# Column sums of the first attention's probabilities: key blocks added on GpSimd, products moved on TensorE

## The chip, the cores and the metric

The kernel runs on one core of a Trainium2 chip. Time is device microseconds of one execution of the whole program. Three runs of the kernel before gave 2255.92, 2256.36 and 2256.59 us (median 2256.36). The engines are TensorE (PE, with PEld for its weight loads), VectorE (DVE), ScalarE (ACT), GpSimd (POOL) and SyncE (SP), which issues the DMAs of this stage.

## The reference, cut to what matters

The program is a decoder block of two cross attentions and two feed-forward parts on x of (8, 256, 512). The change is in the first attention, of 16 heads of 32 over 256 context tokens (of the reference's context only the first 257 rows count as image tokens, and there are 256):

```python
q = rms_norm(linear(x, q_w, q_b), norm_q_w).reshape(B, L, NH, HD)
k_img = rms_norm(linear(ctx_img, k_img_w, k_img_b), norm_k_img_w).reshape(B, -1, NH, HD)
v_img = linear(ctx_img, v_img_w, v_img_b).reshape(B, -1, NH, HD)
...
scores = jnp.einsum('bqhd,bkhd->bhqk', q, k) * scale
probs = jax.nn.softmax(scores, axis=-1)
return jnp.einsum('bhqk,bkhd->bqhd', probs, v)
```

x here is layer-normalised before, and the output is projected, scaled by tanh of a gate and added to x.

## The kernel before

The function is `image_attention` (tiles with the prefix `a_`). It runs in turns, one for a batch i of 256 tokens (two blocks t of 128), for i from -2 to 7. The order on every engine is written out by hand in one loop over the turns; semaphores tie the engines. In the turn of batch i the attention of i is finished while the normalisation, queries, keys and values of i+1 and the keys of i+2 are made.

Projections are three f32 products for each of four parts of 128 (high and low parts of both operands, lines 50 to 52), twelve for a block of 128 tokens and 512 outputs: `queries` (reads a_xt), `values` and `keys` (read a_ctx). The 16 heads are handled in four groups c of four heads (j). `scores` (L740) makes the scores with queries on the partitions, for the maximum (`find_peak`, L1147). `turned_scores` (L755, L758) makes them again with keys on the partitions and takes the maxima off; it fills four double blocks `abc_banks`, so that group c+1 can start only when `exponentials` (L954, ScalarE, two instructions of two heads each) has read group c. The probabilities lie in `a_prob` [128 keys, 2 buffers, 4 heads, 2 key blocks t, 256 queries], buffer c mod 2. `weigh` (L772) multiplies them with the values: 8 products of 32 rows. `masses(i, h, r)` (L782) sums them over the keys with a matrix of ones, `picks_share`; r is the group's place within half h (h = 0: groups 0 and 1; h = 1: groups 2 and 3), and both key blocks are summed by accumulation in the bank m0 or m1, 8 products a group. VectorE inverts the sums (`invert`, L1154, RECIPROCAL 1.75 us), `inverses` (L795) spreads them over the partitions, `divide` (L1159) applies them, ScalarE and GpSimd split the result in a high and a low part (`output_high` L966, `output_low` L614), and `outputs` projects it.

All of these products but the scores and `weigh` go through a ring of three PSUM banks, `a_ring`, in the order of the list PLACES; a user waits until the bank's last user has been read.

What stands in program order around the change:
- ScalarE: exponentials 0, squares of the keys of i+1 (two), exponentials 1, square of query block 0, weight pieces, square of query block 1 (`square_query`, L939), exponentials 2, `output_raw` (L960), weight pieces, `context_high` (L904), exponentials 3, high parts of keys and queries (L920, L924), weight pieces (L976, L982, L984, in the turns up to batch 3 only) and outputs. The pieces are parts of the next stage's weights, made ready here.
- VectorE: low part of x, values' bias (`value`, L1126), statistics of i+2 and a chain of ten tiny instructions for the inverse square roots (`key_scales`: L1096, L1099, L82, and L85, L87, L89 three times, about 0.2 us a step), bias of query block 0 (L1126), `scale_keys` (L1109), `normalise` (L1089) of i+2, bias of query block 1, `query_scales` (L1115 and the like chain), `scale_queries` (L1122), `invert` 0, bias of value block 1, low parts of keys (L1140), `divide` 0, low parts of queries (L1140), `invert` 1.
- GpSimd: `add_row` (L609, two instructions, behind `normalise`), `context_low` (L604), `output_low` twice.

## Time and profile before

| | |
|---|---|
| median of the runs | 2256.36 us |
| the profiled execution, span | 2257.6 us (the page gives no other time of it) |
| PE busy in the span | 2145.6 us, 95% |
| DVE, ACT, POOL busy | 1307.3, 1078.4, 677.1 us |
| first attention | to about 430 us; turned peaks (L721) of batches 0 to 7 at 53.66, 102.67, 159.74, 211.14, 257.56, 304.00, 350.43, 399.04 us |
| L782, the sums | 512 records for 256 products, 0.38 us each, several at a time side by side |

In the page's slices each digit is a tenth of busy time in a fortieth of the span. The first seven slices are this stage: PE 6999998, and PEclk, the granted clock, 9 throughout, since a slice is longer than its dips. A timeline row merges like instructions: its time reaches from the first start to the last end, and the number behind x is the count. Since each f32 product stands in two records, x16 is eight products.

### The profile page before, as it was taken

How to read it: one execution, taken by the hardware profiler on the slowest of the kernel's cores; microseconds unless marked ns; L12 is line 12 of the kernel's file. 1: busy time of each engine (PE TensorE's matmuls, PEld its weight loads, DVE VectorE, ACT ScalarE, POOL GpSimd, SP SyncE). 2: the span in 40 equal slices, each digit the busy share in tenths (PEclk: the TensorE clock that was granted, in tenths of full speed). 3: DMA queues.
4: the chain of work that ended last, by engine and by line, in shares of the span. 5: the costliest groups of instructions: out<-in, count | busy, mean ns of one | idle time of the engine just before them, and what ended most of it. 6: DMA issues, size and time to landing. Idle time of an engine off the chain costs nothing. (4 is left out here: it accounts for less than half of the span.)

```text
span 2257.6 us, 43111 instructions
## 1 busy us (share of the span) xinstructions
PE 2145.6 (95%) x17918; PEld 1788.6 (79%) x17918; DVE 1307.3 (58%) x2283; ACT 1078.4 (48%) x1887; POOL 677.1 (30%) x684
## 2 busy tenths in 40 slices
PE   6999998899999999999999999999799999899996
PEld 5666666444489999999999999999677877799995
DVE  7666776689854445444544444454555455767764
ACT  4676633478744444333433344333455554425553
POOL 4111210266512221111111111211255543125664
PEclk9999999999999999999999999999999999999998
DMA  7454202100032222321223123221000000258995
GB/s 261 160 170 134 81 11 113 57 1 1 29 131 108 89 100 106 112 75 64 86 94 113 64 87 119 79 70 49 25 2 2 2 2 30 85 187 262 275 274 103
DMA packets 46931, 215.30 MB, mean 95 GB/s; under 512 B 6161, under 2 KB 6161, under 8 KB 32401
## 3 DMA queue, kind: packets, MB, share of 16 engines
q1 hardware_dynamic: 29968, 139.13, 17.1%
q0 software_dynamic: 16768, 73.41, 11.3%
q8 instruction: 143, 2.34, 0.4%
q14 instruction: 52, 0.42, 0.1%
HBM read 169.00 MB, written 43.52 MB: 94 GB/s over the span
## 5 line engine op out<-in xcount | busy, mean ns | idle before, releaser
L336 POOL TENSOR_TENSOR c_prob<-c_prob,c_inv_mass 128x512 f32<-128x512 f32 x128 | 130.5, 1039 | 353.1 <-DVE c_inv_mass L328 353.1
L318 ACT ACTIVATE c_prob<-abc_banks,c_neg_peak 128x256 f32<-128x256 f32 x256 | 117.7, 472 | 178.0 <-DVE c_neg_peak L310 178.0
L50 PE MATMUL abc_banks<-c_ctx,c_wk_hi 128*128 128x256 f32 x512 | 146.6, 286 | 2.3 <-DVE c_qt_lo L2148 2.3
L50 PE MATMUL abc_banks<-bc_xt,bc_wq_hi 128*128 128x256 f32 x512 | 147.7, 288 | 0.0
L51 PE MATMUL abc_banks<-bc_xt,bc_wq_hi 128*128 128x256 f32 x512 | 144.9, 283 | 0.0
L52 PE MATMUL abc_banks<-bc_xt,bc_wq_lo 128*128 128x256 f32 x512 | 144.8, 283 | 0.0
L51 PE MATMUL abc_banks<-c_ctx,c_wk_hi 128*128 128x256 f32 x512 | 143.8, 281 | 0.0
L52 PE MATMUL abc_banks<-c_ctx,c_wk_lo 128*128 128x256 f32 x512 | 143.6, 281 | 0.0
L231 PE MATMUL abc_banks<-ab_wq,b_xqt 128*128 128x512 bf16 x512 | 117.2, 380 | 5.8 <-DVE b_h L202 3.7
L1898 POOL DMA_DIRECT2D c_ctx<-kept_scratch x24 | 13.2, 551 | 347.0 <-PE abc_banks L52 347.0
L3220 POOL DMA_INDIRECT out<-el_r,e_target x44 | 82.8, 1882 | 75.6 <-DMA out<-el_r,e_target 60.6
L2150 DVE TENSOR_TENSOR c_v_lo<-abc_banks,c_v_hi 128x512 fp32r<-128x512 f32 x64 | 44.3, 692 | 104.3 <-ACT c_v_hi L2067 104.3
L50 PE MATMUL abc_banks<-c_w_lo,c_o_hi 128*128 128x512 f32 x256 | 102.0, 398 | 2.4 <-DVE c_o_lo L382 2.4
L1343 POOL TENSOR_TENSOR b_hw<-b_h,b_lnw 128x512 f32<-128x512 f32 x64 | 80.9, 1274 | 73.9 <-DVE b_h L202 67.3
L51 PE MATMUL abc_banks<-c_w_hi,c_o_hi 128*128 128x512 f32 x256 | 101.9, 398 | 0.0
L52 PE MATMUL abc_banks<-c_w_hi,c_o_lo 128*128 128x512 f32 x256 | 101.7, 397 | 0.0
L50 PE MATMUL abc_banks<-c_w_lo,c_ctx 128*128 128x512 f32 x256 | 101.7, 397 | 0.0
L52 PE MATMUL abc_banks<-c_w_hi,c_ctx 128*128 128x512 f32 x256 | 101.3, 396 | 0.0
L51 PE MATMUL abc_banks<-c_w_hi,c_ctx 128*128 128x512 f32 x256 | 101.2, 395 | 0.0
L231 PEld LDWEIGHTS abc_banks<-ab_wq,b_xqt 128*128 128x128 bf16 x512 | 47.4, 98 | 66.8 <-DVE b_h L202 12.2
L2067 ACT ACTIVATE c_v_hi<-abc_banks 128x512 fp32r<-128x512 f32 x64 | 38.2, 597 | 127.7 <-PE abc_banks L52 127.7
L50 PEld LDWEIGHTS abc_banks<-c_ctx,c_wk_hi 128*128 128x128 f32 x512 | 96.4, 188 | 2.4 <-issue 2.4
(564 smaller groups left out, 7192.4 us busy)
## 6 DMA issues: line engine op xcount, KB each, us to landing
x_res<-b_w SPq DMA_DIRECT2D x48, 512.0 KB, 4.7
bc_xt<-kept_scratch POOLq DMA_DIRECT2D x24, 1024.0 KB, 5.1
c_ctx<-kept_scratch POOLq DMA_DIRECT2D x24, 1024.0 KB, 5.1
e_raw<-e_w SPq DMA_DIRECT2D x15, 1536.0 KB, 9.2
bc_raw<-c_w SPq DMA_DIRECT2D x16, 1024.0 KB, 4.9
h_res<-e_w SPq DMA_DIRECT2D x7, 1536.0 KB, 9.6
kept_scratch<-bc_xt SPq DMA_DIRECT2D x8, 1024.0 KB, 3.9
kept_scratch<-c_ctx SPq DMA_DIRECT2D x8, 1024.0 KB, 3.9
```

Source lines behind the costliest of these rows:

```text
L50: pe.matmul(out, lhs[0], rhs[1], start=first, stop=False)
L51: pe.matmul(out, lhs[0], rhs[0], start=False, stop=False)
L52: return pe.matmul(out, lhs[1], rhs[0], start=False, stop=last)
L231: mm = pe.matmul(ps[:, k % 2, :], self.xqt[:, n // 2 % 2, c, n % 2, :], w[:, c, self.quarter(k)], start=c == 0, stop=c == C - 1)
L318: ins = act.activation(self.prob[:, u % 2, j, :], self.s_ps[:, j, :], ACT.Exp, bias=self.neg_peak[:, u % 2, j:j + 1], accum_out=self.mass[ ...
L336: pool.tensor_tensor(part, part, self.inv_mass[:, u % 2, js].unsqueeze(2).to_broadcast([P, 2, SEQ]), ALU.mult).then_inc(self.prob_done, 1)
L1343: pool.tensor_tensor(hw[:, n % 2, cols], h[n % 2][:, cols], lnw[:, cols], ALU.mult).then_inc(hw_done, 1)
L1898: pool.dma_start(rows_of(both), kept[1, s % BATCH]).then_inc(ctx_kept_in, 16)
L2067: act.activation(front(k)[0], bank_of(f"f{k}", s), ACT.Copy, scale=SCALE if k < 2 else 1.0).then_inc(front_hi_done, 1)
L2150: ins = dve.tensor_tensor(low, bank_of(f"f{k}", s), f32(high), ALU.subtract)
L3220: pool.indirect_dma_start(out=out[:, :], out_offset=bass.IndirectOffsetOnAxis(ap=target[:, TB * j + t:TB * j + t + 1], axis=0), in_=r[:, j ...
```

## The change

On GpSimd a new function adds, for each group, the probabilities of the two key blocks into `both`, which lies in the tile `a_early_raw` (used only at the start before): two instructions of 128x512 (two heads), each behind the half of the exponential that it reads. `masses` multiplies this sum instead of both blocks: 4 products a group instead of 8. Both groups of a half are now summed at one place: the first half behind the scores of group 3, the second where it was. The wait of the exponentials for a free buffer is now on the additions and the product with the values. The bank of m0 and that of the values' second block change places in the ring, and so do `invert` 0 and the bias of that block on VectorE. Line numbers of the changed kernel are higher by 9 to 20 in this function.

```diff
--- before.py
+++ after.py
@@ -446,6 +446,7 @@
         k_sum, q_sum = sb("k_sum", [P, TB]), sb("q_sum", [P, TB])
         junk = sb("junk", [P, D], BF16)
         raw_v = early_raw[:, :, :, :].rearrange("p a j s -> p (a j s)").rearrange("p (c n) -> p c n", c=C)
+        both = early_raw
         raw = prob[:, :, :, :, :].rearrange("p a j t s -> p a (j t s)").rearrange("p a (c n) -> p a c n", c=C)
         s_ps = handed.s_ps
         x_turned = early.x_bank.bitcast(F16).rearrange("p (c t q) -> p c t q", c=C, t=TB)
@@ -466,7 +467,7 @@
         xn_done, xt_hi_done, k_hat_done, q_hat_done = sem("xn_done"), sem("xt_hi_done"), sem("k_hat_done"), sem("q_hat_done")
         kt_hi_done, qt_hi_done, k_squared, q_squared = sem("kt_hi_done"), sem("qt_hi_done"), sem("k_squared"), sem("q_squared")
         s_ready, peak_done, st_ready, exp_done = sem("s_ready"), sem("peak_done"), sem("st_ready"), sem("exp_done")
-        mass_half, w_ready = sem("mass_half"), sem("w_ready")
+        halves_added, w_ready = sem("halves_added"), sem("w_ready")
         o_raw_done, o_hi_done, o_lo_done = sem("o_raw_done"), sem("o_hi_done"), sem("o_lo_done")
         row_added, x_done, kx_steps, q_steps, stats_done = (
             sem("row_added"), sem("x_done"), sem("kx_steps"), sem("q_steps"), sem("stats_done"))
@@ -481,7 +482,7 @@
 
         TURNS = range(-2, BATCH)
         FIRST_PLACES = (("q0", 1), ("q1", 1), ("v0", 1), ("v1", 1))
-        PLACES = (("mt", 0), ("xt0", 1), ("v0", 1), ("xt1", 1), ("mean", -1), ("q0", 1), ("q1", 1), ("m0", 0), ("v1", 1), ("kt0", 1),
+        PLACES = (("mt", 0), ("xt0", 1), ("v0", 1), ("xt1", 1), ("mean", -1), ("q0", 1), ("q1", 1), ("v1", 1), ("m0", 0), ("kt0", 1),
                   ("kt1", 1), ("n0", 0), ("qt0", 1), ("qt1", 1), ("m1", 0), ("k0", 2), ("n1", 0), ("k1", 2), ("o0", 0), ("o1", 0))
         use_of = {("xt0", 0): 0, ("xt1", 0): 1}
         for i in TURNS:
@@ -613,6 +614,17 @@
                 pool.wait_ge(o_hi_done, 2 * i + h + 1)
                 pool.tensor_tensor(o_lo[:, 2 * h:2 * h + 2, :], o_f[:, :, :], f32(o_hi[:, 2 * h:2 * h + 2, :]),
                                    ALU.subtract).then_inc(o_lo_done, 1)
+
+            def add_halves(i, c):
+
+                n = C * i + c
+                if n >= 2:
+                    await_ready(pool, f"m{(n - 2) % C // 2}", (n - 2) // C)
+                for half in range(2):
+                    js = slice(2 * half, 2 * half + 2)
+                    pool.wait_ge(exp_done, 2 * n + half + 1)
+                    pool.tensor_tensor(both[:, n % 2, js, :], prob[:, n % 2, js, 0, :], prob[:, n % 2, js, 1, :],
+                                       ALU.add).then_inc(halves_added, 1)
 
             pool.memset(eps[:, :], RMS_EPS).then_inc(eps_done, 1)
             pool.memset(ones[:, :], 1.0)
@@ -650,8 +662,14 @@
                     pool.tensor_tensor(w_lo[WO][:, :, :], raw[:, 0], f32(w_hi[WO][:, :, :]), ALU.subtract).then_inc(w_lo_done[WO], 1)
                     pool.wait_ge(row_done, 2)
                     add_row(0)
+                if here(i):
+                    add_halves(i, 0)
+                    add_halves(i, 1)
                 if i >= -1 and here(i + 2):
                     add_row(i + 2)
+                if here(i):
+                    add_halves(i, 2)
+                    add_halves(i, 3)
                 if i >= 0 and here(i + 2):
                     context_low(i + 2)
                 if here(i):
@@ -773,20 +791,16 @@
                                        start=t == 0, stop=t == TB - 1)
                 mm.then_inc(w_ready, 1)
 
-            def masses(i, h, r):
+            def masses(i, h):
 
                 def emit(bank):
-                    n = C * i + 2 * h + r
-                    for t in range(TB):
+                    for r in range(2):
+                        n = C * i + 2 * h + r
+                        pe.wait_ge(halves_added, 2 * n + 2)
                         for j in range(4):
-                            mm = pe.matmul(bank[HD * j:HD * (j + 1), 0:SEQ], share[:, r, :], prob[:, n % 2, j, t, :],
-                                           start=r == 0 and t == 0, stop=r == 1 and t == TB - 1)
+                            mm = pe.matmul(bank[HD * j:HD * (j + 1), 0:SEQ], share[:, r, :], both[:, n % 2, j, :], start=r == 0, stop=r == 1)
                     return mm
-                if r == 0:
-                    pe.wait_ge(ring_free[use_of[f"m{h}", i] % BANKS], use_of[f"m{h}", i] // BANKS)
-                    emit(bank_of(f"m{h}", i)).then_inc(mass_half, 1)
-                else:
-                    use(f"m{h}", i, emit)
+                use(f"m{h}", i, emit)
 
             def inverses(i, h):
 
@@ -840,14 +854,13 @@
                 if i >= 0 and nxt:
                     queries(i + 1, 1)
                 if now:
-                    masses(i, 0, 0)
                     turned_scores(i, 2)
                     weigh(i, 1)
-                    masses(i, 0, 1)
                 if i >= 0 and nxt:
                     values(i + 1, 1)
                 if now:
                     turned_scores(i, 3)
+                    masses(i, 0)
                     weigh(i, 2)
                 if nxt:
                     turn_keys(i + 1, 0)
@@ -861,8 +874,7 @@
                     turn_queries(i + 1, 0)
                     turn_queries(i + 1, 1)
                 if now:
-                    masses(i, 1, 0)
-                    masses(i, 1, 1)
+                    masses(i, 1)
                 if i == BATCH - 1:
                     pe.wait_ge(early.ident_done, 1)
                     early.turn_x(pe, 0, x_turned)
@@ -945,10 +957,7 @@
                     act.wait_ge(w_lo_done[WO], 1)
                 if n >= 2:
                     act.wait_ge(w_ready, n - 1)
-                    if c % 2 == 0:
-                        act.wait_ge(mass_half, n // 2)
-                    else:
-                        await_ready(act, f"m{(n - 2) % C // 2}", (n - 2) // C)
+                    act.wait_ge(halves_added, 2 * (n - 1))
                 for half in range(2):
                     js = slice(2 * half, 2 * half + 2)
                     act.activation(prob[:, n % 2, js], s_ps[:, js], ACT.Exp).then_inc(exp_done, 1)
@@ -1233,10 +1242,10 @@
                     scale_queries(i + 1)
                 if i == -1:
                     value(i + 1, 0)
+                if nxt:
+                    value(i + 1, 1)
                 if now:
                     invert(i, 0)
-                if nxt:
-                    value(i + 1, 1)
                 if nxt:
                     low("kt", i + 1, 0, kt_lo, kt_hi, kt_hi_done)
                     low("kt", i + 1, 1, kt_lo, kt_hi, kt_hi_done)
```

TensorE, from the end of the scores of group 3 in the turn of batch 0 to the second half's sums. Before:

```order
L758 MATMUL abc_banks<-a_peak_t,picks_pick 128x256 x4
L772 MATMUL a_o_ps<-a_prob,a_v 32x256 x8
L674 MATMUL a_ring<-ident,a_kf 128x128 x4
L772 MATMUL a_o_ps<-a_prob,a_v 32x256 x8
L674 MATMUL a_ring<-ident,a_kf 128x128 x4
L795 MATMUL a_ring<-a_inv_mass,picks_spread 128x256 x2
L674 MATMUL a_ring<-ident,a_qf 128x128 x8
L782 MATMUL a_ring<-a_prob,picks_share 32x256 x16
```

Now, where L801 is `masses`, L790 `weigh`, L773 and L776 `turned_scores`, L692 the turned keys and queries and L809 `inverses`:

```order
L776 MATMUL abc_banks<-a_peak_t,picks_pick 128x256 x4
L801 MATMUL a_ring<-a_early_raw,picks_share 32x256 x8
L790 MATMUL a_o_ps<-a_prob,a_v 32x256 x8
L692 MATMUL a_ring<-ident,a_kf 128x128 x4
L790 MATMUL a_o_ps<-a_prob,a_v 32x256 x8
L692 MATMUL a_ring<-ident,a_kf 128x128 x4
L809 MATMUL a_ring<-a_inv_mass,picks_spread 128x256 x2
L692 MATMUL a_ring<-ident,a_qf 128x128 x8
L801 MATMUL a_ring<-a_early_raw,picks_share 32x256 x8
```

The sums of groups 0 and 1 stand in one group of 8 in front of `weigh` of group 2, and the 16 products of the second half are 8. (Before, 8 each stood in front of and behind the scores of group 2.)

GpSimd, one turn (the row additions of i+2 to the next). Before:

```order
L609 TENSOR_TENSOR x_res<-x_res,a_row 128x512 [waits a_xn_done]
L609 TENSOR_TENSOR x_res<-x_res,a_row 128x512
L604 TENSOR_TENSOR a_ctx_lo<-a_ctx_f,a_ctx_hi 128x1024 [waits a_ring_ready,a_ctx_hi_done]
L614 TENSOR_TENSOR a_o_lo<-a_o_f,a_o_hi 128x512 [waits a_o_hi_done] x2
L609 TENSOR_TENSOR x_res<-x_res,a_row 128x512 [waits a_xn_done]
```

Now, from group 0's additions on, where L626 are the additions, L610 `add_row`, L605 `context_low` and L615 `output_low`:

```order
L626 TENSOR_TENSOR a_early_raw<-a_prob 128x512 [waits a_exp_done,a_ring_ready]
L626 TENSOR_TENSOR a_early_raw<-a_prob 128x512 [waits a_exp_done]
L626 TENSOR_TENSOR a_early_raw<-a_prob 128x512 [waits a_exp_done,a_ring_ready]
L626 TENSOR_TENSOR a_early_raw<-a_prob 128x512 [waits a_exp_done]
L610 TENSOR_TENSOR x_res<-x_res,a_row 128x512 [waits a_xn_done]
L610 TENSOR_TENSOR x_res<-x_res,a_row 128x512
L626 TENSOR_TENSOR a_early_raw<-a_prob 128x512 [waits a_exp_done,a_ring_ready]
L626 TENSOR_TENSOR a_early_raw<-a_prob 128x512 [waits a_exp_done]
L626 TENSOR_TENSOR a_early_raw<-a_prob 128x512 [waits a_exp_done,a_ring_ready]
L626 TENSOR_TENSOR a_early_raw<-a_prob 128x512 [waits a_exp_done]
```

Four additions stand in front of the row additions and four between them and the low part of the context. The third and fourth group's wait for the ring (a_ring_ready) too, for the first half's sums, which read the buffer that they write.

## Rows read from the trace of the kernel before

**Rows 1.** Busy time by engine in one stretch of the first attention (us, x instructions).

```profile
250.00:300.00 50.00, 48.53 (x514) 34.92 (x510) 36.35 (x59) 21.45 (x32) 8.24 (x6) 1.00 0.13 43
```

**Rows 2.** TensorE's waits, batches 0 to 7: total us, times, longest.

```profile
PE a_o_ps L772 <- ACT a_prob L954: 5.1, 8, 1.4
```

**Rows 3.** Timeline of TensorE, batch 4: start, us, line, tiles, count, [idle before].

```profile
271.25 1.07 PE L782 MATMUL a_ring<-a_prob,picks_share 128*32 128x256 f32 x16
272.25 0.39 PE L755 MATMUL abc_banks<-a_qt_hi,a_kt_lo 32*128 32x256 f32 x4
...
274.29 1.05 PE L782 MATMUL a_ring<-a_prob,picks_share 128*32 128x256 f32 x16
275.26 0.50 PE L50 MATMUL a_ring<-ab_wq,a_ctx_hi 128*128 128x512 f32 x1
...
278.26 0.39 PE L755 MATMUL abc_banks<-a_qt_hi,a_kt_lo 32*128 32x256 f32 x4
...
281.52 1.07 PE L772 MATMUL a_o_ps<-a_prob,a_v 128*32 128x256 f32 x16 [0.45 <-ACT a_prob L954]
...
285.24 1.93 PE L782 MATMUL a_ring<-a_prob,picks_share 128*32 128x256 f32 x32
287.11 0.39 PE L740 MATMUL abc_banks<-a_kt_lo,a_qt_hi 32*128 32x256 f32 x4
```

**Rows 4.** Timeline of ScalarE, batch 4.

```profile
267.38 1.94 ACT L954 ACTIVATE a_prob<-abc_banks 128x1024 f32<-128x1024 f32 x2 [0.70 <-PE abc_banks L758]
...
273.31 0.63 ACT L939 ACTIVATE a_junk<-a_qf 128x512 bf16<-128x512 f32 x1 [2.11 <-DVE a_qf L1126]
...
273.94 1.92 ACT L954 ACTIVATE a_prob<-abc_banks 128x1024 f32<-128x1024 f32 x2
...
278.43 1.06 ACT L904 ACTIVATE a_ctx_hi<-a_ctx_f 128x1024 fp32r<-128x1024 f32 x1 [2.08 <-PE a_ring L52]
279.53 1.94 ACT L954 ACTIVATE a_prob<-abc_banks 128x1024 f32<-128x1024 f32 x2
```

**Rows 5.** Timeline of VectorE, batch 4.

```profile
268.56 0.17 DVE L85 TENSOR_TENSOR a_kx_tmp<-a_kx_rstd 128x4 f32<-128x4 f32 x1
...
269.74 0.69 DVE L1126 TENSOR_TENSOR a_qf<-a_ring,a_row 128x512 f32<-128x512 f32 x1
...
272.59 0.69 DVE L1126 TENSOR_TENSOR a_qf<-a_ring,a_row 128x512 f32<-128x512 f32 x1
274.06 1.24 DVE L1115 SCALAR_TENSOR_TENSOR a_q_var<-a_q_sum,a_eps 128x2 f32<-128x2 f32 x1 [0.79 <-ACT a_junk L939]
...
285.15 1.52 DVE L1140 TENSOR_TENSOR a_qt_lo<-a_ring,a_qt_hi 128x512 fp32r<-128x512 f32 x2
```

**Rows 6.** Timeline of GpSimd, batch 4.

```profile
272.75 2.54 POOL L609 TENSOR_TENSOR x_res<-x_res,a_row 128x512 f32<-128x512 f32 x2 [21.98 <-DVE a_xn L1089]
279.56 2.37 POOL L604 TENSOR_TENSOR a_ctx_lo<-a_ctx_f,a_ctx_hi 128x1024 fp32r<-128x1024 f32 x1 [4.28 <-ACT a_ctx_hi L904]
```

**Rows 7.** Timelines of VectorE and GpSimd, 9 to 12.5 us.

```profile
9.32 1.28 DVE L87 SCALAR_TENSOR_TENSOR a_kx_tmp<-a_kx_tmp,a_kx_var 128x4 f32<-128x4 f32 x1
10.63 1.20 DVE L89 SCALAR_TENSOR_TENSOR a_kx_rstd<-a_kx_tmp,a_kx_rstd 128x4 f32<-128x4 f32 x1
...
9.32 2.49 POOL L642 TENSOR_TENSOR a_ctx_lo<-a_ctx_f,a_ctx_hi 128x512 fp32r<-128x512 f32 x2
```

**Rows 8.** Timeline of ScalarE, batch 3.

```profile
233.18 1.92 ACT L954 ACTIVATE a_prob<-abc_banks 128x1024 f32<-128x1024 f32 x2
```

**Rows 9.** Timeline of TensorE, two waits of batches 2 and 6.

```profile
184.65 1.07 PE L772 MATMUL a_o_ps<-a_prob,a_v 128*32 128x256 f32 x16 [1.39 <-ACT a_prob L954]
...
390.72 0.79 PE L50 MATMUL a_ring<-a_w_lo,a_o_hi 128*128 128x512 f32 x1 [1.60 <-POOL a_o_lo L614]
...
395.23 0.39 PE L740 MATMUL abc_banks<-a_kt_lo,a_qt_hi 32*128 32x256 f32 x4
```

**Rows 10.** Busy time and granted clock behind the second of them.

```profile
392.00:394.00 2.00, 2.00 (x6) 1.52 (x6) 0.00 (x0) 0.00 (x0) 0.00 (x0) 0.50 0.00 0
```


## The prediction

> **What bounds the kernel now.** I read the stretches of the span first, then TensorE's waits, then the timelines of one turn of the first attention (batch 4's, from its turned peaks at 257.56 us on) for TensorE, ScalarE, VectorE and GpSimd, and last the places where VectorE and GpSimd meet. The change touches the first attention alone, up to about 430 us. In a steady stretch of it TensorE is busy 48.53 of 50 us and GpSimd 8.24 [rows 1], so a product taken from TensorE is time, unless what it feeds comes later. TensorE's wait for a finished exponential, 5.1 us in eight turns, is the one that the change works next to [rows 2]. In the turn of batch 4 the reader is to see how tight two places are. (a) The third scores start at 278.26 [rows 3]; they need the third exponential, which ScalarE runs from 273.94 to 275.86 (two halves, 1.92) straight behind the square of the queries at 273.31, and that waits for VectorE's biased queries at 272.59 [rows 4, 5]. (b) The next scores start at 287.11, only 0.44 us behind the end of the last low part of the queries on VectorE, 285.15 + 1.52 = 286.67 [rows 3, 5]. Behind (b) the turn runs as now, whatever came before it.
>
> **What is taken from TensorE.** Each column sum was 8 products (16 records) over both key blocks and becomes 4 (8 records). The first two sums take 272.25 - 271.25 = 1.00 and 275.26 - 274.29 = 0.97 us, the last two together 287.11 - 285.24 = 1.87 [rows 3]. Sixteen records for two sums then cost 0.97 both times: 1.00 + 0.97 - 0.97 = 1.00 in the first part of a turn, 1.87 - 0.97 = 0.90 in the second, 1.90 a turn, 15.2 us over eight. That is the ceiling if nothing waits.
>
> **Where the moved products stand.** Without the two sums in front, TensorE is ready for the third scores at 278.26 - 1.00 - 0.97 = 276.29. These need the third exponential's end, 275.86 now: 0.4 to spare. The first two sums now stand behind them, in the stretch in which TensorE waited 0.45 for the last exponential [rows 3].
>
> **What GpSimd adds.** Eight additions of 128x512 a turn. Its row addition of that shape and type took 2.54 for two, 1.27 each [rows 6]; the nearest other row is the low part of the context, 2.37 for twice the elements, 1.19 [rows 6]. I take 1.27, 10.2 us a turn; the rows' own ends are 1.19 and 1.27, and only more than these would matter (a rival below). GpSimd has the room; the question is who else is held. No DMA is issued or moved.
>
> **The addition and VectorE.** Where GpSimd begins an addition while VectorE is in its chain of tiny instructions on two SBUF operands, they stop: at 9.32 GpSimd runs two back to back for 2.49, and VectorE's 0.16 us instructions take 1.28 and 1.20, one behind each [rows 7]. In batch 4's turn the query-scale instruction at 274.06, as tiny as those, takes 1.24, till GpSimd's row additions end at 275.29 [rows 5, 6]. Now look where the second exponential's additions fall. It starts at 267.38, its halves end at about 268.40 and 269.32 [rows 4]; additions run 268.4 to 269.7 and to 270.95. VectorE's inverse square root is in its middle then: the step at 268.56 would wait till 269.7, the next till 270.95, and the rest follows as now; at 0.2 a step, the step of 268.96 stands at 271.0. The chain ends 2.0 us late, and with it the biased queries (269.74, then 272.59 becomes 274.6), the square (275.35), and the third exponential (276.0 to 277.9) [rows 4, 5]. TensorE, ready at 276.3, waits 1.6 us at the third scores and starts them at 277.95 instead of 278.26.
>
> **Rule beside it.** The Trainium skill (SBUF — State Buffer, Who interferes with whom) says that a VectorE instruction with two SBUF inputs and a GpSimd one that reads SBUF exclude each other for the whole instruction, and one with an input in PSUM is free. The rows at 9.32 agree for the first half. It would also let VectorE's f32 scalings hold off GpSimd, which no row here shows; the sum below leaves that out.
>
> **The turns.** Batches 4 and 5: third scores 277.95 to 279.1, context part on ScalarE 278.4 to 279.45, last exponential at 279.45 against 279.53 [rows 4], the sums fill the gap, the last product with values at 281.5 against 281.52. Nothing won so far. The third and fourth additions wait until the first sums are through (280.1, for the buffer): 280.1 to 285.3, just in time for the second pair of sums at 285.24 + 0.5, and context's low part ends at 287.6. At (b) the low queries end as now, so the new gain is 0.44 of the 0.90. I take -0.5 each. Batches 0, 2 and 3: between the third exponential and the last one ScalarE also does the weight pieces and the context (batch 3's last exponential starts at 233.18 with no idle time in front, behind both [rows 8]), so the 2.0 us pass through to the last exponential and to (b): 2.0 - 0.44 = +1.6 each; in 0 and 2 ScalarE's pieces behind it carry nearly all of it, +1.8 and +2.1. Batch 1's chain is over before its second exponential ends; it wins a part of the first 1.0: -0.7 (estimate). Batch 6 has no tokens left to normalise, its exponential stays in time, and both gains arrive: -2.2 (1.90 and part of the 0.45). Batch 7 has no other work: each addition stands in the path, and what the 1.90 brings they mostly take: -0.5 (estimate). Sum: 1.8 - 0.7 + 2.1 + 1.6 - 0.5 - 0.5 - 2.2 - 0.5 = +1.1 us. The profiled execution's span is 2257.6 us, 1.2 over the median of the runs, 2256.36; the change is read from the one and put on the other: 2257.5.
>
> **Rivals.**
> *Chain not held (faster).* If VectorE's chain slips through (additions begin a step later, or only one step is held), batches 4 and 5 win 0.44 + 1.6 = 2.1 each, 6 wins 2.5, 0, 2, 3 win 0.44 each (ScalarE still sets the last exponential), 1 and 7 win 1.0 each: -10.0, 2246.3. For it: at the meeting point the two start within 0.2 us of each other, and a step that comes first is through. Against: the instructions at 9.32, 10.63 and 274.06 all waited in full, and six more steps follow.
> *The clock falls (slower).* The place is the new 1.6 us wait in front of the third scores. A wait of 1.60 was followed by half clock, products at 390.72 on taking 4.51 till 395.23 against 278.26 - 275.26 = 3.00 for twelve at full clock [rows 3, 9], granted clock 0.50, which is 1.2 GHz [rows 10]; a wait of 1.39 alone was not (1.07 for 16 records, as ever) [rows 9]. Price 1.5 each. It decides if the new waits count as the 1.60 did: in batches 4 and 5 in full, in 0, 2, 3 partly behind ScalarE: 3.0 + 4.5 x 0.6 = +5.7, in all +6.8, 2263.2.
> *GpSimd comes late (slower).* The additions are queued ahead of the low context, and that ahead of the low outputs; the keys product waits for the context. My sum leaves 0.1 to 0.4 us there. At 1.6 us an addition (each held off by VectorE's scalings) four cost 1.3 more, in batches 4 to 7 in full: +5, 2262.5.
>
> **Numbers.** Forecast 0.45 (own range 2253 to 2261.5), chain not held 0.23, clock 0.20, GpSimd late 0.12. 0.2% is 4.5 us, about what a measurement can tell. Faster: the second case and a rest of the first, 0.25; within: most of the first, a fifth of the last two, 0.45; slower 0.30. The range takes in the -10 case at its edge and the clock case: 2246 to 2265.
>
> **What would show it.** Right: 128 products for the sums instead of 256; five turns in which a 128x4 step of VectorE takes 1.2 us twice just behind the second exponential; a wait of TensorE for the exponential in front of the third scores (none there now) of 1.6 us; turns of 46.4 us still at 46, batch 3's longer by 1.6, batch 6's shorter by 2. Wrong: those steps at 0.16 us throughout (then the time falls by 10), half clock behind the new waits, or the keys products waiting for the low context.

## The result, and the profile of the changed kernel

The changed kernel takes 2270.89 us in the median of four runs (2264.82 to 2273.48), the kernel before 2256.14 beside it (2255.68 to 2256.59): a ratio of 1.0059, with a 95% interval of 1.0045 to 1.0073. Measured once more later, with twelve runs, it is 2264.46 against 2256.91, 1.0031 (1.0018 to 1.0044). So it is slower, by some 7 to 15 us; the forecast of 2257.5 was too low, and the first measurement lies above its range, which ended at 2265. The second lies just inside, with a change of 7.6 us where 1.1 was forecast.

The span of the profiled execution is 2271.8 us, 14.2 more than before. ScalarE and TensorE run the same instructions at both kernels' ends, so the two traces can be laid on each other. I read two marks: where the first attention ends (the last of its output products but one starts) and how long the last stage, the experts, takes (ScalarE's first to last write of `el_r`). The first attention ends at 436.25 instead of 429.34, +6.9. Between there and the last stage both take 1620.4. The last stage, whose code is not touched, takes 196.15 instead of 189.66, +6.5; 0.8 more lie behind its last write. Two causes, then; the first is that of the change.

Busy time in the stretch of [rows 1], in the changed kernel:

```profile
250.00:300.00 50.00, 47.22 (x497) 34.46 (x494) 39.26 (x60) 24.91 (x35) 18.12 (x14) 1.00 0.27 84
```

TensorE has lost 1.3 us of work and GpSimd has gained 10. TensorE's waits over the first attention, of which [rows 2] showed the third kind:

```profile
PE abc_banks L773 <- ACT a_prob L963: 12.6, 8, 2.1
PE a_ring L50 <- POOL a_o_lo L615: 10.0, 6, 5.1
PE a_o_ps L790 <- ACT a_prob L963: 6.3, 5, 1.9
```

The first of them, turned scores that wait for an exponential, was 2.2 us in two waits before. Now batch 4's turn, which starts at 266.28 here. VectorE and GpSimd, as in [rows 5, 6]:

```profile
277.06 0.16 DVE L89 SCALAR_TENSOR_TENSOR a_kx_rstd<-a_kx_tmp,a_kx_rstd 128x4 f32<-128x4 f32 x1
277.26 1.27 DVE L85 TENSOR_TENSOR a_kx_tmp<-a_kx_rstd 128x4 f32<-128x4 f32 x1
278.56 1.22 DVE L87 SCALAR_TENSOR_TENSOR a_kx_tmp<-a_kx_tmp,a_kx_var 128x4 f32<-128x4 f32 x1
279.82 0.16 DVE L89 SCALAR_TENSOR_TENSOR a_kx_rstd<-a_kx_tmp,a_kx_rstd 128x4 f32<-128x4 f32 x1
...
283.45 0.68 DVE L1135 TENSOR_TENSOR a_qf<-a_ring,a_row 128x512 f32<-128x512 f32 x1
```

```profile
277.21 2.55 POOL L626 TENSOR_TENSOR a_early_raw<-a_prob 128x512 f32<-128x512 f32 x2 [1.96 <-ACT a_prob L963]
283.61 2.52 POOL L610 TENSOR_TENSOR x_res<-x_res,a_row 128x512 f32<-128x512 f32 x2 [3.85 <-DVE a_xn L1098]
289.10 4.98 POOL L626 TENSOR_TENSOR a_early_raw<-a_prob 128x512 f32<-128x512 f32 x4 [2.97 <-ACT a_prob L963]
294.03 2.40 POOL L605 TENSOR_TENSOR a_ctx_lo<-a_ctx_f,a_ctx_hi 128x1024 fp32r<-128x1024 f32 x1
```

Two steps of VectorE's chain wait one addition each, exactly as the prediction placed them; the second biased queries stand 17.17 us into the turn instead of 15.03. The third exponential and TensorE follow (ScalarE as in [rows 4], TensorE as in [rows 3]):

```profile
284.17 0.63 ACT L951 ACTIVATE a_junk<-a_qf 128x512 bf16<-128x512 f32 x1 [2.11 <-DVE a_qf L1135]
...
284.80 1.92 ACT L963 ACTIVATE a_prob<-abc_banks 128x1024 f32<-128x1024 f32 x2
```

```profile
286.76 0.39 PE L773 MATMUL abc_banks<-a_qt_hi,a_kt_lo 32*128 32x256 f32 x4 [1.62 <-ACT a_prob L963]
...
287.92 1.07 PE L801 MATMUL a_ring<-a_early_raw,picks_share 128*32 128x256 f32 x16
...
295.66 0.39 PE L758 MATMUL abc_banks<-a_kt_lo,a_qt_hi 32*128 32x256 f32 x4 [0.50 <-DVE a_qt_lo L1149]
```

TensorE waits 1.62 us before the third scores, and the turn is 46.0 us long instead of 46.4.

The lengths of the eight turns (from one batch's turned peaks to the next's, the last to the end mark), over two executions of each kernel:

| | b0 | b1 | b2 | b3 | b4 | b5 | b6 | b7 | end of first attention | last stage |
|---|---|---|---|---|---|---|---|---|---|---|
| before | 49.0 | 57.1 | 51.4 | 46.4 | 46.4 | 46.4 | 48.6 | 30.3 | 429.3 | 189.7 |
| before, again | 48.9 | 56.6 | 50.5 | 46.4 | 46.4 | 46.4 | 48.8 | 28.9 | 427.1 | 195.4 |
| changed | 49.7 | 58.3 | 56.0 | 48.1 | 46.0 | 46.1 | 46.6 | 31.4 | 436.3 | 196.2 |
| changed, again | 49.9 | 58.7 | 55.3 | 49.5 | 46.1 | 46.1 | 46.2 | 29.6 | 433.9 | 189.7 |
| change of the means | +0.8 | +1.7 | +4.7 | +2.4 | -0.4 | -0.3 | -2.3 | +0.9 | +6.9 | |
| predicted | +1.8 | -0.7 | +2.1 | +1.6 | -0.5 | -0.5 | -2.2 | -0.5 | +1.1 | |

The ends differ by 0.5 us less than the sum of the turns (+7.4), because the first peaks start at 53.66 and 54.19 before and at 54.20 and 52.53 in the changed kernel. Batches 4, 5 and 6 came out as predicted, batch 0 is 1.0 better and batch 3 0.8 worse. Batches 1, 2 and 7 make most of the 6 us that the sum missed.

The same eight turns can be split by what TensorE does: idle, or busy, and of its busy time what the granted clock cost it (each busy stretch times one minus the clock granted in it). In the means of two traces each:

| | idle | lost to the clock while busy | the rest |
|---|---|---|---|
| before | 28.2 | 14.1 | 332.0 |
| changed | 47.1 | 18.0 | 316.6 |
| change | +18.9 | +3.9 | -15.4 |
| predicted | +16.3 (1.1 + 15.2) | 0 | -15.2 |

The work that was taken away is what was predicted. The miss is 3.9 us of clock and 2.6 of waiting. Batch 1, VectorE and GpSimd:

```profile
121.16 0.69 DVE L1135 TENSOR_TENSOR a_qf<-a_ring,a_row 128x512 f32<-128x512 f32 x1
121.76 3.17 DVE L1118 SCALAR_TENSOR_TENSOR a_kf<-a_kf,a_kx_rstd,a_row 128x512 f32<-128x512 f32 x2
```

```profile
121.38 3.01 POOL L626 TENSOR_TENSOR a_early_raw<-a_prob 128x512 f32<-128x512 f32 x2 [4.19 <-ACT a_prob L963]
```

The chain is over there when the second exponential ends, as I had said; but the two scalings of the keys stand behind it, and they take 3.17 instead of 1.41 (two of 0.74, one starting 0.66 behind the other), and the additions 3.01 instead of 2.55: each engine waits for the other. Batch 2 of the changed kernel, ScalarE and behind it GpSimd and TensorE:

```profile
202.56 1.15 ACT L993 ACTIVATE x_res<-x_res,a_shifts 128x1024 bf16<-128x1024 f32 x1
205.57 1.24 ACT L991 ACTIVATE x_res<-x_res,a_shifts,a_inv_mean 128x1024 f32<-128x1024 f32 x1 [1.86 <-DMA x_res<-b_w]
206.85 1.15 ACT L993 ACTIVATE x_res<-x_res,a_shifts 128x1024 bf16<-128x1024 f32 x1
207.90 0.61 ACT L975 ACTIVATE a_o_hi<-a_o_f 128x512 fp32r<-128x512 f32 x1
```

```profile
208.59 1.26 POOL L615 TENSOR_TENSOR a_o_lo<-a_o_f,a_o_hi 128x512 fp32r<-128x512 f32 x1 [7.88 <-ACT a_o_hi L975]
```

```profile
209.91 0.80 PE L50 MATMUL a_ring<-a_w_lo,a_o_hi 128*128 128x512 f32 x1 [5.05 <-POOL a_o_lo L615]
```

A weight piece (`x_res<-b_w`) has not landed when ScalarE asks for it, and the high output, its low part and TensorE's last products are queued behind. Before, ScalarE went from one piece to the next without a gap there, and TensorE's wait was 2.75. The piece is not late because ScalarE is: between the issue of its load and ScalarE's asking for it lie 4.64 us here (199.07 to 203.71) and 4.56 before (193.94 to 198.50). The load itself took 6.5 us instead of 4.4.

### The profile page after: what moved, and what is told of

It reads as the page before. It is cut to its first block and busy times, and to the rows that moved or that the text cites. A ratio compares the mean times of both kernels' runs of the same rounds, so it can differ in the third digit from the quotient of the medians.

```text
span 2271.8 us, 42690 instructions
## 1 busy us (share of the span) xinstructions
PE 2134.3 (94%) x17643; PEld 1784.7 (79%) x17662; DVE 1324.1 (58%) x2283; ACT 1077.3 (47%) x1887; POOL 756.5 (33%) x748
## 5 line engine op out<-in xcount | busy, mean ns | idle before, releaser
L626 POOL TENSOR_TENSOR a_early_raw<-a_prob 128x512 f32<-128x512 f32 x64 | 80.9, 1291 | 161.0 <-ACT a_prob L963 148.7
L1352 POOL TENSOR_TENSOR b_hw<-b_h,b_lnw 128x512 f32<-128x512 f32 x64 | 80.9, 1274 | 74.8 <-DVE b_h L202 67.4
```

Source lines behind the costliest of these rows:

```text
L626: pool.tensor_tensor(both[:, n % 2, js, :], prob[:, n % 2, js, 0, :], prob[:, n % 2, js, 1, :], ALU.add).then_inc(halves_added, 1)
L1352: pool.tensor_tensor(hw[:, n % 2, cols], h[n % 2][:, cols], lnw[:, cols], ALU.mult).then_inc(hw_done, 1)
```

## The experiments

Ends and turns are read as in the table above, each from one profiled execution; the ratios are to the kernel before on the same chip.

**Additions of the second group behind the row addition.** On GpSimd:

```diff
                     add_halves(i, 0)
-                    add_halves(i, 1)
                 if i >= -1 and here(i + 2):
                     add_row(i + 2)
                 if here(i):
+                    add_halves(i, 1)
                     add_halves(i, 2)
```

> The changed kernel, with the additions of the second head group queued behind GpSimd's row addition instead of ahead of it; nothing else. Theory (held chain): GpSimd's additions hold VectorE's inverse square root for 2.0 us in batches 0, 2, 3, 4 and 5, and with it the third exponential. Here the additions stand some 7 us later, when that chain is over: its steps take 0.16 us, the wait of 1.6 us in front of the third scores is gone in batches 4 and 5, and the first attention ends 8 to 12 us sooner than in the changed kernel. Rival (GpSimd is late, or the products' new place costs): nothing is sooner, the first sums wait more, the end moves by +2 to -2. Last stage: it grew by 6.5 us in the changed kernel; if that comes from what the new sums round to, it stays here (time 2259 to 2263); if it comes from when the stage is reached or from chance, it may be gone (2252 to 2256).

Measured: 2293.4 us, ratio 1.0159 (1.0114 to 1.0204); the first attention ends at 465.3, 29 us later than in the changed kernel. Batch 4's turn is 53.1 us. Neither theory had this; VectorE's timeline has where it starts, and GpSimd's beside it.

```profile
296.31 1.25 DVE L1124 SCALAR_TENSOR_TENSOR a_q_var<-a_q_sum,a_eps 128x2 f32<-128x2 f32 x1 [0.79 <-ACT a_junk L951]
297.59 1.23 DVE L82 TENSOR_SCALAR a_q_rstd<-a_q_var 128x2 int32<-128x2 int32 x1
298.85 1.21 DVE L85 TENSOR_TENSOR a_q_tmp<-a_q_rstd 128x2 f32<-128x2 f32 x1
...
303.53 1.18 DVE L89 SCALAR_TENSOR_TENSOR a_q_rstd<-a_q_tmp,a_q_rstd 128x2 f32<-128x2 f32 x1
304.75 3.93 DVE L1131 TENSOR_SCALAR a_qf<-a_qf,a_q_rstd 128x512 f32<-128x512 f32 x2
```

```profile
295.00 2.54 POOL L610 TENSOR_TENSOR x_res<-x_res,a_row 128x512 f32<-128x512 f32 x2 [6.20 <-DVE a_xn L1098]
297.49 2.55 POOL L626 TENSOR_TENSOR a_early_raw<-a_prob 128x512 f32<-128x512 f32 x2
300.96 4.95 POOL L626 TENSOR_TENSOR a_early_raw<-a_prob 128x512 f32<-128x512 f32 x4 [0.92 <-PE a_ring L801]
305.88 2.51 POOL L605 TENSOR_TENSOR a_ctx_lo<-a_ctx_f,a_ctx_hi 128x1024 fp32r<-128x1024 f32 x1
```

The first chain is free here (0.16 us a step), and the third exponential in time. But the queries have a chain of their own, 16.5 us into a turn, which I had left out: six of its steps wait for an addition (the first for one of the rows, as before), and the two scalings of the queries, which read one SBUF tile and a scalar, take 3.93 instead of 0.89. TensorE then waits 6.1 us in this turn for what VectorE has queued behind them (27.3 us over five turns). Part of the 29 us is clock: while TensorE is busy it loses 33.8 us to it in the eight turns, against 19.6 in the changed kernel's first trace. So a hold costs what is behind it; a later place is not a safer one.

**The additions alone.** The kernel before, with `add_halves` and its places as in the change (result unused), and in `exponentials`:

```diff
                     act.wait_ge(w_ready, n - 1)
+                    act.wait_ge(halves_added, 2 * (n - 1))
```

> The kernel before, with GpSimd's additions put in where the changed kernel has them, their result unused, and the exponentials waiting for them as there; products and order on TensorE as before. Theory (held chain): the third exponential comes 2.0 us late; TensorE still has its two sums in front of the third scores, so batches 4 and 5 lose little (0 to 0.5), batches 0, 2 and 3, where ScalarE sets the last exponential, 1.6 to 2.1 each: the first attention ends 5 to 8 us later than before. Rival (the additions cost nothing by themselves, the order of the products does): no more than +1. Last stage: the sums are the same as before, so if it grows with what the sums round to it is as before (total 2261 to 2264); if it grows from the time at which it is reached, it is longer here too (2266 to 2271).

Measured: 2286.07 us, ratio 1.0129 (1.0096 to 1.0161); the end is at 454.9, 26 us later than before, not 5 to 8. Half of the theory holds (the first chain loses its two steps), but without the sums' bank to wait for, GpSimd takes up the third group's additions as soon as the third exponential ends, which is in the second chain: it is over 28.1 us into the turn instead of 19.7. In the changed kernel a wait that I had priced at nothing, for the first sums before the third group's additions, keeps them out of that chain. Here too the clock is a part: 23.9 us lost while busy, against 14.5. The last stage took 189.7, though it was reached late.

**No additions.** The changed kernel with GpSimd's part and all waits on it taken out, and:

```diff
-                        pe.wait_ge(halves_added, 2 * n + 2)
+                        pe.wait_ge(halves_added, 1)
```

> The changed kernel without the additions: the 128 products for the sums read a tile that GpSimd fills once with a constant, and nothing waits for additions. What is left out: the real sums of the probabilities. Theory (held chain): TensorE keeps its 1.90 us a turn and VectorE's chain is free: turns of 44.3 us in batches 4 and 5 instead of 46.4, the first attention ends 8 to 12 us sooner than in the kernel before and 15 to 19 sooner than in the changed one. Rival (the order or the banks of the products cost): the end stays within 4 us of the kernel before. The last stage isn't compared, since other numbers reach its routing.

Measured: 2258.54 us, ratio 1.0011 (0.999 to 1.0031). The end is at 425.6, only 3.8 us sooner than before, which by its number is the rival's outcome, and 10.7 sooner than in the changed kernel. But its turns start 4.3 us later (the first peaks at 57.93 instead of 53.66; GpSimd's one fill of the whole tile is the only new work ahead of them), and together they are 8.1 us shorter than in the first trace of before. Batches 4 and 5 take 45.5, not 44.3. The low part of the context now starts 20.1 us into the turn instead of 22.0, and meets the scaling of the queries:

```profile
279.65 3.06 DVE L1115 TENSOR_SCALAR a_qf<-a_qf,a_q_rstd 128x512 f32<-128x512 f32 x2
```

```profile
280.05 2.38 POOL L605 TENSOR_TENSOR a_ctx_lo<-a_ctx_f,a_ctx_hi 128x1024 fp32r<-128x1024 f32 x1 [2.42 <-ACT a_ctx_hi L901]
```

The same hold, by an instruction that has always been there. Batch 2 takes 52.4 us, more than before: its weight piece is late as well (6.2 us for the load, 1.5 of ScalarE's wait), though nothing holds the chain. The last stage took 199.3, but other numbers reach it.

**Fills in place of additions.**

```diff
-                    pool.tensor_tensor(both[:, n % 2, js, :], prob[:, n % 2, js, 0, :], prob[:, n % 2, js, 1, :],
-                                       ALU.add).then_inc(halves_added, 1)
+                    pool.memset(both[:, n % 2, js, :], 2.0).then_inc(paced, 1)
+                    pool.wait_ge(paced, 2 * n + half + 1)
+                    pool.memset(both[:, n % 2, js, :], 2.0).then_inc(halves_added, 1)
```

> The changed kernel with each addition of 128x512 replaced by two fills of the same 128x512 piece of the tile, 0.53 us each: GpSimd has the same queue, the same waits and writes, and is busy some 1.1 to 1.2 us for each instead of 1.27, but reads nothing from SBUF. What is left out: the real sums. Theory (held chain, by GpSimd's reading against VectorE's instructions with two SBUF operands): VectorE's steps are free or held by less, and the first attention ends as without the additions, within 3 us. Rival (GpSimd is late, or everything waits for its queue): it ends as in the changed kernel, within 3 us. A third outcome: writes hold VectorE as reads do, then the steps take 0.5 us or more and the end is between.

Measured: 2249.41 us, ratio 0.998 (0.9958 to 1.0002). Batches 4 and 5 take 44.37, and the end is at 416.1: 20 us before the changed kernel's, and 9.5 before that of the run without additions, not within 3 of it (6 of the 9.5 lie ahead of the first peaks). In the chain of batch 4:

```profile
262.92 0.16 DVE L89 SCALAR_TENSOR_TENSOR a_kx_rstd<-a_kx_tmp,a_kx_rstd 128x4 f32<-128x4 f32 x1
263.12 0.16 DVE L85 TENSOR_TENSOR a_kx_tmp<-a_kx_rstd 128x4 f32<-128x4 f32 x1
```

```profile
262.79 0.53 POOL L627 MEMSET a_early_raw<- 128x512 f32 x1 [2.68 <-ACT a_prob L965]
```

GpSimd is nearly as busy (1.1 us instead of 1.27 for each), in the same queue with the same waits, and writes the same tile, and VectorE's steps take 0.16. So neither GpSimd's queue nor its writes hold the steps with two SBUF operands; what the addition does besides, and the fill does not, is to read SBUF. The rule of the Trainium skill (SBUF — State Buffer, Who interferes with whom) that they meet only where the GpSimd instruction reads agrees. It also takes GpSimd's lateness out as a cause. Over the eight turns this kernel is 10.1 us shorter than the mean of before, which is the total that the rival "chain not held" had worked out (-10.0). In batches 4, 5 and 6 that is its mechanism (-2.0, -2.0 and -2.4 against 2.1, 2.1 and 2.5); the rest agrees by luck, since batch 1 wins 3.5 where it had 1.0, and batch 2 loses 1.9 where it had a gain of 0.4. Batch 2 has the late piece again (6.5 us for the load, a wait of 1.8), with its exponentials in time.

**The second group's sum by products.** Only the first, third and fourth group are added; the first sums stand in front of the last turned scores.

```diff
+                        if n % C == 1:
+                            for t in range(TB):
+                                for j in range(4):
+                                    mm = pe.matmul(bank[HD * j:HD * (j + 1), 0:SEQ], share[:, r, :], prob[:, n % 2, j, t, :],
+                                                   start=False, stop=t == TB - 1)
+                            continue
...
+                    masses(i, 0)
                     turned_scores(i, 3)
-                    masses(i, 0)
```

> The changed kernel, but the second head group isn't added by GpSimd: its sum takes 8 products over both key blocks as before, the other three groups 4 each; both first sums stand in front of the last turned scores. Theory (only the second group's additions meet VectorE's first chain, 11 us into a turn; those of groups 1, 3 and 4 stand beside instructions that read PSUM): the steps there take 0.16 us again, the third exponential is in time, batches 0 and 3 to 5 are 0.4 to 1.5 us shorter than before, the first attention ends 2 to 8 us before that of the kernel before and 9 to 15 before the changed kernel's. Rival (the other additions, the order or the weight pieces' DMAs cost as well): the end is at or behind the kernel before. The last stage should be 189.7 or some 196 us, whichever chance gives.

Measured: 2253.18 us, ratio 0.9981 (0.997 to 0.9993); turns of 48.1, 54.1, 51.2, 45.9, 45.4, 45.5, 47.3 and 28.8, the end at 418.9: 17 us before the changed kernel's first trace and 10 before that of before, both more than expected. The chain's steps take 0.16 throughout, and TensorE's waits for exponentials are short again:

```profile
PE a_ring L50 <- POOL a_o_lo L616: 8.5, 7, 3.2
PE a_o_ps L792 <- ACT a_prob L974: 5.4, 8, 1.1
PE abc_banks L760 <- DVE a_qt_lo L1160: 3.5, 7, 0.5
```

The eight turns together take 366.4 us, 15.3 less than in the changed kernel and 2.2 more than with fills, though TensorE has four products more in each. Two of the eight additions of a turn, then, carry the loss; the sums' place was moved as well, and I did not try that alone. Batch 2 has no wait of 5 us here either, because the load of its piece took 4.9 us and had landed when ScalarE asked. That is not owed to exponentials in time: they are so in the last two runs too, and there it was late.

**Small pieces.** The second group's two additions cut into eight of 128x128:

```diff
+                    if c == 1:
+                        for j in (2 * half, 2 * half + 1):
+                            for part_of in (slice(0, SEQ // 2), slice(SEQ // 2, SEQ)):
+                                ins = pool.tensor_tensor(both[:, n % 2, j, part_of], prob[:, n % 2, j, 0, part_of],
+                                                         prob[:, n % 2, j, 1, part_of], ALU.add)
```

> The changed kernel with the second group's two additions of 128x512 cut into eight of 128x128 each 0.3 to 0.45 us. Theory (a step of VectorE waits for the addition that runs, and GpSimd's next one is in before VectorE's next step): two waits of 1.2 us become six to eight of 0.3 to 0.4; each still lets one step through, so the chain loses 0.9 to 1.6 us instead of 2.1, and the first attention ends 2 to 6 us sooner than in the changed kernel. Rival (the chain waits till GpSimd's queue is empty): nothing is won, or it is longer by the pieces' fixed costs.

Measured: 2257.99 us, ratio 1.0002 (0.9989 to 1.0015), the end at 431.4, 5 us sooner than the first trace of the changed kernel. Batches 4 to 6 win; batches 1 and 2 (58.9 and 55.5) do not.

```profile
276.52 0.46 DVE L85 TENSOR_TENSOR a_kx_tmp<-a_kx_rstd 128x4 f32<-128x4 f32 x1
277.01 0.39 DVE L87 SCALAR_TENSOR_TENSOR a_kx_tmp<-a_kx_tmp,a_kx_var 128x4 f32<-128x4 f32 x1
277.43 0.39 DVE L89 SCALAR_TENSOR_TENSOR a_kx_rstd<-a_kx_tmp,a_kx_rstd 128x4 f32<-128x4 f32 x1
```

```profile
276.50 3.39 POOL L629 TENSOR_TENSOR a_early_raw<-a_prob 128x128 f32<-128x128 f32 x8 [1.98 <-ACT a_prob L970]
```

One step passes behind each piece, as the theory said: six waits of 0.2 to 0.3, 1.4 us in all, and TensorE waits 0.85 at the third scores instead of 1.62. The hold is by instruction.

**The changed kernel again**, unchanged.

> The changed kernel once more, unchanged. If the 6.5 us that its last stage took longer in the first trace were chance of that execution, the last stage is 189 to 191 us here and the time 2262 to 2266; if they belong to this kernel, 196 again and 2269 to 2273. The first attention should end at 436 within 1 us in both.

Measured: the 2264.46 us given at the start, the end at 433.9 (2.3 sooner than in the first trace, more than I had allowed), the last stage 189.7.

**Row additions last.** The version with the second group by products, and GpSimd's two row additions behind its low outputs.

```diff
                     output_low(i, 1)
+                if i >= 0 and here(i + 2):
+                    add_row(i + 2)
```

> The version without the second group's additions, and GpSimd's two row additions of a turn queued behind its low outputs instead of in the middle. Theory (a GpSimd instruction that reads SBUF holds VectorE's next step on SBUF operands until it ends): the step at 16.5 us into a turn, which waits 1.24 us in every kernel so far, takes 0.16, and the second chain ends 1.07 us sooner. TensorE waits there for the last exponential (0.45) and the low queries (0.50), not for that chain, so turns of batches 4 and 5 stay at 45.4 within 0.3; in all 0 to 3 us sooner than that version. Rival (that hold is on the path): 0.8 to 1.1 us a turn, 6 to 9 in all.

Measured: 2254.08 us, ratio 0.9993 (0.9974 to 1.0012). The step that took 1.24 us in all kernels so far takes 0.16:

```profile
269.92 0.16 DVE L1137 SCALAR_TENSOR_TENSOR a_q_var<-a_q_sum,a_eps 128x2 f32<-128x2 f32 x1 [0.79 <-ACT a_junk L961]
```

Batches 4 and 5 stay at 45.47: that hold is off the path, and the rival falls. The end, 420.2, is no sooner: batch 2 takes 53.8, with a wait of 4.5 at its output products and a load of 5.2 us for its piece, again with the chain free.

**A weight piece behind the high output.** The changed kernel, in the table of the pieces' places:

```diff
-    PLACES_OF_STEPS = {-1: (0, 0, 1, 1, 4), 0: (2, 1, 2, 4, 9), 1: (1, 1, 2, 2, 5), 2: (1, 1, 2, 2, 2), 3: (1, 1, 0, 1, 2)}
+    PLACES_OF_STEPS = {-1: (0, 0, 1, 1, 4), 0: (2, 1, 2, 4, 9), 1: (1, 1, 2, 2, 5), 2: (1, 1, 2, 1, 3), 3: (1, 1, 0, 1, 2)}
```

> The changed kernel, with one weight piece of batch 2 that ScalarE rounds moved behind its second high output. Theory (in batch 2 the changed kernel loses more than VectorE's chain explains, because that piece's DMA lands 1.9 us after ScalarE asks for it, and the high output, its low part on GpSimd and TensorE's last products are queued behind it): batch 2's turn is 1.9 to 3.2 us shorter (TensorE's gap in front of the output products 5.1 becomes 2 to 3), the end of the first attention as much sooner, 432 to 434. Rival (the high output itself is late, by VectorE or the clock): no change in that turn, within 0.5.

Measured: 2260.09 us, ratio 1.0022 (1.0003 to 1.004). TensorE's gap in front of batch 2's output products is 0.80 instead of 5.05, and the turn 50.1 instead of 56.0 and 55.3: more than expected, since a whole piece of 2.4 us went as well as its wait. Batch 3 gives 2 us back (51.0 against 48.1 and 49.5, with a new gap of 1.4 at its start). The end is at 431.0. So ScalarE's queue in front of the high output sets the end of this turn. How much of the 5.6 us is the late load the run does not tell, since the piece's own work left the place too; the load took 6.2 us here as well.

**The kernel before again**, unchanged.

> The kernel before once more, for the scatter between executions: its first attention should end at 429.3 within 1.5 us; the last stage takes 189.7, or some 6 to 10 us more where a scatter of rows lands late, whatever the kernel.

Measured: 2261.19 us, ratio 1.001 (0.9996 to 1.0025); the end at 427.1, 2.3 sooner than in its first trace and more than the 1.5 that I had allowed, the last stage 195.4. So a long last stage comes with the kernel before as well.

**Both together.** The second group by products, and in that table `1: (1, 1, 2, 1, 6), 2: (1, 1, 2, 1, 3)`.

> The version without the second group's additions, and in batches 1 and 2 one weight piece moved behind ScalarE's second high output. Theory (a piece of 2.4 us in front of that output is on the path to TensorE's last products, whose gaps are 3.2 us in both turns): gaps of 0.8 to 1.0, both turns 2.2 shorter, less what the pieces give back later; the first attention ends 1 to 4.5 us before the 418.9 of that version, the time is 2248 to 2252. Rival (the pieces' DMAs bound these batches, and what is won there is lost in the next turn): within 1 us of 418.9.

Measured: 2251.04 us, ratio 0.9977 (0.9961 to 0.9993), the end at 418.5: within 0.5 us of the version without the moved pieces. The gaps at the outputs shrink and others grow:

```profile
PE abc_banks L775 <- ACT a_peak_t L930: 8.5, 3, 4.2
PE a_ring L50 <- POOL a_o_lo L616: 4.5, 7, 1.6
```

8.5 and 4.5 us against 5.2 and 8.5. That is the rival's outcome: what a turn wins is lost at the start of the next. Whether the pieces' DMAs are what it waits for I did not try. By ratio and by median this is the fastest version that computes the sums, 0.2% below the kernel before; its interval overlaps that of the version before it almost fully.

## Why the prediction was wrong

*The bound and TensorE's saving* were right: batch 6, which has no chain to hold, is 2.3 us shorter (predicted 2.2), and batches 4 and 5 are 0.3 to 0.4 shorter (0.5).

*The hold* was right in place, size and reach in batches 4 and 5: two steps of 1.27 and 1.22 us, the biased queries 2.14 late, a wait of 1.62 at the third scores (1.6 predicted). That it is what costs is shown three ways: take away GpSimd's reads (fills), those two additions (products), or their length (pieces), and the time comes back in the same order (ends at 416.1, 418.9 and 431.4).

*Batch 1* is the first step that failed: "its chain is over before its second exponential ends; it wins a part of the first 1.0". I had only asked whether the additions meet the chain. They meet the next two instructions, scalings of 128x512, which hold GpSimd as well. That is the term that the prediction named ("it would also let VectorE's f32 scalings hold off GpSimd") and set at nothing, because no row showed it. The turn is +1.7 instead of -0.7: TensorE idles 2.6 us more, 1.3 of it at the last exponential, and loses 1.2 more to the clock. A part of the idle time stands ahead of the second group's additions, at the turned peaks (3.45 and 3.95 us instead of 2.75 and 2.24), and stays unexplained. The version without the second group's additions wins 2.7 in that turn against the mean of before.

*Batch 2* is the second, and the largest of a single turn, +4.7 instead of +2.1. I carried the 2.0 us through ScalarE to (b) and stopped there. Behind (b) ScalarE had a weight piece queued in front of the high output, and I took for granted that its DMA had landed, as it had before; ScalarE waits 1.9 and 2.0 us for it. TensorE idles 5.5 us more than before, where my sum had 4.0, and loses 1.1 more to the clock. "Behind it the turn runs as now" is true of batches 4 and 5 and not of a turn in which ScalarE also feeds on DMAs. Moving the piece took 5.2 to 5.9 us from the turn. Why its load takes longer is open. It took 6.1 to 6.7 us in both traces of the changed kernel, with the second group behind the rows, without additions, with fills, with small pieces and with the moved piece, and 4.3 to 5.2 in the others, which are both traces of before, the additions alone and the versions by products. The held chain is on both sides of that list, so it is not the cause; the changed place or number of the products may be, which I did not try.

*The clock* is the third step that failed, and the largest term: the sum had it at nothing, and it is 3.9 us of the 6.5. The rival had a price for it, at the new wait in front of the third scores. In batches 4 and 5 that is refuted: over the wait of 1.62 us and the products behind it, the granted clock is 1.00.

```profile
283.00:290.00 7.00, 5.38 (x76) 3.55 (x75) 5.83 (x18) 5.81 (x8) 3.42 (x3) 1.00 0.01 2
```

But batches 2 and 3 have that wait and one of 1.9 for the last exponential 5.6 us behind it, and there half clock (1.2 GHz) did follow, in batch 2 of the first trace (TensorE, and the stretch from 189 us on) and in batch 3 of the second (granted 0.50 from 243 to 246 us):

```profile
188.50 1.16 PE L790 MATMUL a_o_ps<-a_prob,a_v 128*32 128x256 f32 x16 [1.88 <-ACT a_prob L963]
```

```profile
189.00:192.00 3.00, 3.00 (x20) 2.23 (x13) 1.28 (x2) 0.60 (x1) 3.00 (x3) 0.56 0.60 175
```

Before, the clock was 1.00 there in both traces. The same two waits in batch 3 of the first trace and batch 2 of the second were not followed by it, so whether it comes is not settled by their length. (The wait of 1.60 from which the prediction took its price had one of 3.11 us ahead of it, at 384.07, which it did not show.) The changed kernel also runs more at half clock at the end of batch 1, where TensorE had waited 3.22 (2.75 before), 0.53 against 0.82 in the same stretch:

```profile
153.00:159.00 6.00, 6.00 (x32) 4.38 (x36) 0.66 (x1) 5.41 (x6) 0.00 (x0) 0.53 0.87 281
```

At 0.29 of the clock over 6 us that is 1.7 us by an estimate. In the five runs without the held chain the loss is 10.7 to 12.1 us instead of 18.0. Batch 7 is 0.9 longer instead of 0.5 shorter, 0.6 of it clock, but both kernels scatter by 1.4 to 1.7 us there.

*The last stage* was in no term. In 13 profiled executions it took 189.6 to 190.9 us ten times, and 195.4 (before), 196.2 (changed) and 199.3 (without additions) three times. In the first trace of the changed kernel it builds up over several places where a scatter of rows lands late; the longest wait of GpSimd is:

```profile
2152.44 2.32 POOL L3229 DMA_INDIRECT out<-el_r,e_target  x1 [0.30 <-issue]
...
2164.79 1.62 POOL L3229 DMA_INDIRECT out<-el_r,e_target  x1 [7.43 <-DMA out<-el_r,e_target]
```

In that stretch the scatters land within 8.6 us in the second trace of the changed kernel; one takes 12.1 in the first. I had read the run-to-run scatter off three runs that lay within 0.7 us; in the later measurements the same kernel went from 2249.8 to 2266.3. A range drawn around a median has to hold that, and mine did not. What makes a scatter land late, and whether it happens more often in one kernel than in the other, stays open; so does how much of the 14.8 us of the first measurement is that. The change itself is worth +6.9 us at the end of the first attention, which agrees with the second measurement's 7.6. Put on 2256.4 it gives 2263, close to the clock rival's 2263.2, but that is luck: the rival had the clock in batches 4 and 5, where it stayed full, and no late piece.

The rival "GpSimd comes late" took its price from additions of 1.6 us; their mean is 1.29 (80.9 us for 64), and no keys product waits for the context.

## What to carry to other kernels

Before moving work to GpSimd, lay its instructions over VectorE's timeline in every kind of turn, and look at all instructions of VectorE with SBUF operands in that stretch, not at the one chain that is known to suffer; what is free in one turn is held in another, and a later place may be worse. Price a new wait of TensorE also by the clock that may be lost behind it. Where a late result passes through an engine that also consumes DMAs, follow it to the end of that engine's queue. And when two instructions of a large set carry the loss, leave those two out: with three quarters of the additions the kernel was 0.2% faster than before.

## What the runs showed of the hardware

- A GpSimd instruction that reads SBUF holds a VectorE instruction with two SBUF operands until it ends (1.27 and 1.22 us for 0.16), one that only writes does not (0.16).
- It holds VectorE's f32 scalings with one SBUF tile and a scalar too: 3.93 and 3.06 us for two that take 0.89. VectorE's instructions with an operand in PSUM beside the additions kept their times (0.68 to 0.69 for 128x512).
- VectorE's 128x512 scalings hold GpSimd as well: two additions took 3.01 us instead of 2.55.
- Between two queued GpSimd additions one VectorE step passed, at both lengths tried: eight additions of 128x128 (0.42 each, against 1.27 for four times the elements) let six steps through at 0.4 each.
- Two waits of TensorE in one turn, of 1.7 to 1.9 us and of 1.9, 5.6 us apart, were followed by half clock in two of four such turns; single waits of 1.62 us were not (granted 1.00).
- The load of one weight piece, asked for by ScalarE 4.6 us after its issue, took 4.4 us in one kernel and 6.5 in another; the cause is open.
- The scatter of rows in the last stage landed 4.6 to 12.1 us after its issue in the first trace of the changed kernel; that stage was 5.7 to 9.6 us longer in three of 13 executions.
